# Two-layer perceiver block on one Trainium2 core: in the first head of each quad of cross attention, value projections placed in steps 3 to 8, and the splits and weighings reordered around them

## The reference, cut to what matters

```python
x = x + xattn(layernorm(x), ctx, Wq, Wk, Wv, Wo)      # x: [256, 512], ctx: [4096, 512]

def xattn(inputs_q, inputs_kv, Wq, Wk, Wv, Wo):       # H = 16 heads of HD = 128
    q = (inputs_q @ Wq).reshape(b, sq, H, HD) / sqrt(HD)
    k = (inputs_kv @ Wk).reshape(b, skv, H, HD)
    v = (inputs_kv @ Wv).reshape(b, skv, H, HD)
    attn = softmax(einsum('bqhd,bkhd->bhqk', q, k))
    return einsum('bhqk,bkhd->bqhd', attn, v).reshape(b, sq, H * HD) @ Wo
```

## Time and profile before

| | us |
|---|---|
| median of three runs | 1710.48 |
| lowest, highest | 1710.27, 1711.05 |
| the profiled execution | 1707.27 |
| its span, first to last instruction | 1705.5 |
| TensorE busy | 1649.8 (97%) |
| VectorE busy | 1090.5 (64%) |
| ScalarE busy | 694 (41%) |
| mean granted TensorE clock | 0.994 |

### The profile page before, as it was taken

How to read it: one execution, slowest core, us unless ns; L and a number is a source line. 1 busy time by engine, 2 the same in 40 slices (tenths; PEclk the granted TensorE clock), 3 DMA queues, 4 the chain that set the end, 5 groups by cost and what they waited for, 6 DMA issues and landing times.

```text
span 1705.5 us, 23514 instructions
## 1 busy us (share of the span) xinstructions
PE 1649.8 (97%) x9232; PEld 1296.6 (76%) x9232; DVE 1090.5 (64%) x1754; ACT 693.8 (41%) x938; POOL 126.6 (7%) x213
## 2 busy tenths in 40 slices
PE   8998999999999999999999999999889999999998
PEld 7887888888788888888888878888657646644444
DVE  4445777777777777777777788896554923633333
ACT  3334444544444444444444455554221312222221
POOL 0000000000000000000000001001000000011110
PEclk9999999999999999999999999999989999999999
DMA  6755454445554554545445543226210519199991
GB/s 222 206 173 152 130 136 130 126 129 137 138 140 124 136 130 123 147 136 130 121 131 140 132 120 97 93 81 216 81 50 1 197 56 421 60 381 395 396 381 48
DMA packets 117293, 270.41 MB, mean 159 GB/s; under 512 B 7168, under 2 KB 76992, under 8 KB 111040
## 3 DMA queue, kind: packets, MB, share of 16 engines
q1 hardware_dynamic: 96512, 194.45, 36.2%
q0 software_dynamic: 20672, 74.46, 14.6%
HBM read 200.69 MB, written 68.19 MB: 158 GB/s over the span
## 4 chain that ended last, share of the span: by engine, by line
PE 61%; issue 27%; DVE 4%; DMA 3%; POOL 3%; ACT 2%; SPq 0%; POOLq 0%; DVEq 0%; ACTq 0%
PE bank L41 14%; PE bank L390 13%; PE bank L362 9%; PE bank L1921 5%; PE bank L403 5%; PE bank L1551 3%; PE bank L1942 2%; PE bank L1941 2%; DMA v_dram<-v_out 2%; PE bank L1950 2%; POOL v_back L887 1%; PE bank L1906 1%; PE bank L135 1%; DMA v_out<-in_wv 1%; PE bank L1096 1%
## 5 line engine op out<-in xcount | busy, mean ns | idle before, releaser
L716 DVE TENSOR_TENSOR e_lo<-S,e_hi 128x1024 fp32r<-128x1024 f32 x128 | 156.5, 1223 | 88.8 <-ACT e_hi L548 88.4
L362 PE MATMUL bank<-cT_hi,wk_hi 128*128 128x512 f32 x512 | 205.6, 402 | 0.0
L390 PE MATMUL bank<-wv_hi,cT_hi 128*128 128x512 f32 x512 | 199.8, 390 | 3.5 <-DVE wv_lo L653 3.5
L362 PE MATMUL bank<-cT_hi,wk_lo 128*128 128x512 f32 x512 | 200.6, 392 | 0.0
L539 ACT ACTIVATE S<-S 128x1024 f32<-128x1024 f32 x128 | 135.7, 1060 | 159.6 <-DVE S L696 159.5
L390 PE MATMUL bank<-wv_hi,cT_lo 128*128 128x512 f32 x512 | 199.5, 390 | 0.0
L362 PE MATMUL bank<-cT_lo,wk_hi 128*128 128x512 f32 x512 | 199.2, 389 | 0.0
L390 PE MATMUL bank<-wv_lo,cT_hi 128*128 128x512 f32 x512 | 199.2, 389 | 0.0
L548 ACT CAST e_hi<-S 128x1024 fp32r<-128x1024 f32 x128 | 134.7, 1052 | 145.0 <-PE bank L403 141.0
L709 DVE TENSOR_TENSOR esum<-esum,S 128x512 f32<-128x512 f32 x210 | 145.0, 690 | 72.0 <-ACT S L539 68.4
L403 PE MATMUL bank<-e_hi,v_back 128*128 128x256 f32 x880 | 166.1, 286 | 8.3 <-DVE small L734 4.3
(11 more groups left out here) (280 smaller groups left out, 2851.7 us busy)
## 6 DMA issues: line engine op xcount, KB each, us to landing
w<-in_w_moe SPq DMA_DIRECT2D x32, 2304.0 KB, 11.6
v_dram<-v_out SPq DMA_DIRECT2D x112, 512.0 KB, 4.5
v_back<-v_dram POOLq DMA_DIRECT2D x110, 512.0 KB, 4.9
v_dram<-v_back SPq DMA_DIRECT2D x16, 512.0 KB, 3.9
ctx_nat<-in_ctx SPq DMA_DIRECT2D x8, 1024.0 KB, 4.9
ctx_raw<-in_ctxT SPq DMA_DIRECT2D x7, 1024.0 KB, 8.0
v_late<-v_dram POOLq DMA_DIRECT2D x14, 512.0 KB, 3.5
l_w_qkv<-in_l_wqkv SPq DMA_DIRECT2D x6, 1024.0 KB, 7.4
```

The costliest lines, as they stand in the source:

```text
L362: t = e.matmul(banks[b][:], l, r, start=(c == 0 and m == 0), stop=(c == DT - 1 and m == 2))
L390: t = e.matmul(banks[b][:], l, r, start=(c == 0 and m == 0), stop=(c == DT - 1 and m == 2))
L716: e.tensor_tensor(lo[:], Sj, hi[:].bitcast(F32), ALU.subtract).then_inc(e_split, 1)
```

## The change

In the first head of each quad (`starts_quad(h)`: h = 0, 4, 8) the units are spread differently over the steps: none in steps 0 and 1, two in step 2, one each in steps 3 to 6, two in step 7. The number of units, and every operation's work, is as before. In these heads the orders change as well:

- TensorE: `weigh(h, j-1)` comes behind `project_k(h+1, j)` and ahead of the unit, from step 3 on; `weigh(h, 1)` stands between the two units of step 2; `finish_head(h-1)` comes ahead of the scores of step 0. In h = 0 `weigh(0, 0)` comes behind the scores of step 1.
- ScalarE: `round_wv` of pieces 0 and 1 comes behind `round_e(h, 0)` and `raise_scores(h, 1)`; in each later step `round_k` and `store_scores` come ahead of `round_e`; pieces 2 and 3 come behind `raise_scores(h, 2)`.
- VectorE: `split_wv` of pieces 0 and 1 comes behind `split_e(h, 0)`, that of pieces 2 and 3 behind `keep_max(h+1, 0)`; `split_k` comes first in each step; `invert_sum(h-1)` comes earlier and `add_head(h-1)` later.

Other heads keep their order.

```diff
@@ -257,7 +257,13 @@
                 return []
             s = h % HPQ * NCH + j
             first = (h // HPQ + 1) * KVT
-            return [] if s == 0 else [first, first + 1] if s == 1 else [first + s]
+            if s < 2:
+                return []
+            return [first + u for u in ((0, 1) if s == 2 else (6, 7) if s == 7 else (s - 1,) if s < 7 else (s,))]
+
+        def starts_quad(h):
+
+            return h < LATE and h % HPQ == 0
 
         def sync_cross(e):
             def load_qo(n):
@@ -447,17 +453,23 @@
                     project_q(1)
             for h in range(LATE):
                 for j in range(NCH):
-                    if j >= 2:
+                    if j == 0 and h:
+                        weigh(h - 1, NCH - 1)
+                    elif j >= 2 and not starts_quad(h):
                         weigh(h, j - 1)
-                    elif j == 0 and h:
-                        weigh(h - 1, NCH - 1)
                     project_k(h + 1, j)
-                    if j == 1:
-                        weigh(h, 0)
-                    for u in units(h, j):
+                    if j == 0 and h and starts_quad(h):
+                        finish_head(h - 1)
+                    if h and j == 1 or j >= 3 and starts_quad(h):
+                        weigh(h, j - 1)
+                    for m, u in enumerate(units(h, j)):
                         project_v(u)
+                        if j == 2 and starts_quad(h) and m == 0:
+                            weigh(h, 1)
                     scores(h + 1, j)
-                    if j == 0 and h:
+                    if h == 0 and j == 1:
+                        weigh(0, 0)
+                    if j == 0 and h and not starts_quad(h):
                         finish_head(h - 1)
                     if j == NCH // 2:
                         project_q(h + 2)
@@ -593,22 +605,26 @@
                         for u in units(h, 0):
                             round_v(u)
                         raise_scores(h, 0)
-                        if h % HPQ == 0:
+                        round_e(h, 0)
+                        raise_scores(h, 1)
+                        if starts_quad(h):
                             round_wv(h // HPQ + 1, 0)
                             round_wv(h // HPQ + 1, 1)
-                        round_e(h, 0)
-                        raise_scores(h, 1)
                         continue
-                    if j == 1:
-                        round_k(h + 1, 1)
-                        if h % HPQ == 0:
-                            round_wv(h // HPQ + 1, 2)
-                            round_wv(h // HPQ + 1, 3)
+                    if j == 1 or starts_quad(h):
+                        round_k(h + 1, j)
+                    if starts_quad(h):
+                        store_scores(h + 1, j - 1)
                     round_e(h, j)
-                    store_scores(h + 1, j - 1)
-                    if j > 1:
-                        round_k(h + 1, j)
-                    if j == NCH - 1:
+                    if not starts_quad(h):
+                        store_scores(h + 1, j - 1)
+                        if j > 1:
+                            round_k(h + 1, j)
+                    if j == 1 and starts_quad(h):
+                        raise_scores(h, 2)
+                        round_wv(h // HPQ + 1, 2)
+                        round_wv(h // HPQ + 1, 3)
+                    elif j == NCH - 1:
                         round_wk(h + 2)
                     else:
                         raise_scores(h, j + 1)
@@ -780,27 +796,38 @@
                         for u in units(h, 0):
                             split_v(u)
                         shift(h, 1)
-                        if h % HPQ == 0:
+                        if h and starts_quad(h):
+                            invert_sum(h - 1)
+                        sum_e(h, 0)
+                        split_e(h, 0)
+                        if starts_quad(h):
                             split_wv(h // HPQ + 1, 0)
                             split_wv(h // HPQ + 1, 1)
-                        sum_e(h, 0)
-                        split_e(h, 0)
-                        if h:
+                        elif h:
                             invert_sum(h - 1)
                         continue
                     if j == 1:
+                        if h and not starts_quad(h):
+                            add_head(h - 1)
+                        if starts_quad(h):
+                            split_k(h + 1, 1)
+                            sum_e(h, 1)
+                        else:
+                            sum_e(h, 1)
+                            split_k(h + 1, 1)
+                        shift(h, 2)
+                    elif starts_quad(h):
+                        split_k(h + 1, j)
+                    split_e(h, j)
+                    keep_max(h + 1, j - 1)
+                    if j == 1 and starts_quad(h):
+                        split_wv(h // HPQ + 1, 2)
+                        split_wv(h // HPQ + 1, 3)
                         if h:
                             add_head(h - 1)
-                        sum_e(h, 1)
-                        split_k(h + 1, 1)
-                        if h % HPQ == 0:
-                            split_wv(h // HPQ + 1, 2)
-                            split_wv(h // HPQ + 1, 3)
-                        shift(h, 2)
-                    split_e(h, j)
-                    keep_max(h + 1, j - 1)
                     if j > 1:
-                        split_k(h + 1, j)
+                        if not starts_quad(h):
+                            split_k(h + 1, j)
                         if j + 1 < NCH:
                             shift(h, j + 1)
                     if j == NCH - 1:
```

## The result

The changed kernel takes 1720.63 us (median of four runs, 1718.72 to 1722.95) against 1710.76 us (median of four): ratio 1.0058, 95% interval 1.0046 to 1.0071, 9.9 us slower. The profiled execution had 1719.85 us, its span is 1718.0 us.

A forecast was written before the change was run, and what follows sets the result against it. TensorE was taken to bound the loop: gaps of 17.9 against 14.2 us (+3.7) plus slow clock (+2.6) gave +6.3 us on the median of 1710.5, so 1716.8 us, range 1708 to 1721.

The forecast's parts named there:

- What bounds the kernel: TensorE sets the loop's time; only its gaps, 14.2 us in all, can be won by a new order.
- Part 1: Steps 0 and 1: idle TensorE of 1.56, 2.6 and 0.1 us in head 0, 0.45 us in heads 4, 8.
- Part 2: Step 2's pair of units makes step 3's scores 3.9 us late (2.8 to 5.0) in heads 0, 4, 8.
- Part 3: Pair of units in step 7: the next scores 0.35 us late per head (0 to 2), where it was 0.
- Sum of the gaps: TensorE's gaps together: 17.9 us against 14.2, +3.7 us (about +0.4 to near +12).
- The clock: Slow clock behind gaps over 2.5 us: three more such gaps, half followed by 1.7 us loss, +2.6 us (0 to 6.8).
- the pair did not stay hidden: Rival claimed step 2's pair stays hidden, step 3's scores in time: -8 us, 1702.5; chance 0.11.
- trade evenly: Rival: transfers of 3.6 to 4.4 us and a clock that holds; +0.4 to +3.4 us, about 1712.5; chance 0.27.
- near case: First unit's transfer in step 2, issued close to a load of values: taken as 4.7 us (ends 3.6 and 5.8).
- the transfers alone: Transfers with no load of values close by: 4.1 and 3.6 us; 4.1 taken for step 7.
- the estimate of 3.2 us: 512 KB DMA: about 2 us plus bytes over 436 GB/s; would shorten step 3's gaps 1.5 us each, sum +1.8.

The follow-up runs named there:

- Experiment 1: Changed kernel with the round and split of the pair's second unit moved from step 2 into step 3 (heads 0, 4, 8): 1706.99 us.
- experiment 2: Changed kernel with 10 identity matmuls on TensorE ahead of the scores of step 3 in heads 0, 4, 8: 1715.02 us.
- experiment 8: Kernel before the change with 9 identity matmuls ahead of the scores of step 1 in heads 12, 13, 14: 1706.8 us.
- experiment 5: Changed kernel with the whole series of units rounded and split one place later in heads 0, 4, 8: 1708.01 us.
- experiment 3: Kernel before the change with only the new list of units, all orders as they were: 1721.22 us.
- experiment 4: Kernel of experiment 3 with step 1 mended in heads 0, 4, 8: scores copied right behind the keys' round, keys split first: 1725.01 us.
- changed kernel again: The changed kernel itself, unaltered, measured again beside the kernel before: 1720.65 us, ratio 1.0067.

## Why the prediction was right, and which term was too small

1716.8 us was forecast, with slower as the likeliest, and 1720.63 measured, inside the range of 1708 to 1721. It held narrowly: two of the four runs lie above 1721, and the likeliest band of 1714 to 1720.5 is just missed. The gaps came out as reasoned; the clock did not.

- **What bounds the kernel:** right. The gaps of TensorE and its slow clock give 9.8 of the loop's 10.8 us.
- **Part 1:** right to a few tenths. Head 0's new gap was put at 2.6 us and is 2.82 + 0.16; 0.45 for heads 4 and 8 are 0.48 + 0.16. The waits for wv_lo went. The load for head 0's second weighing (0.1 in the sum) cost nothing. A weighing late in the loop still waits 0.5 us for v_back, as one did for 0.3 before.
- **Part 2, the pair in step 2:** right. The weighing starts at 158.41 and the first unit is in v_out at 167.95, w + 9.5 (9.6 forecast); the transfer took 4.4 us (4.7 taken); the scores start at w + 16.2 (16.4). The gap is 3.7 us with its 0.16 (3.9). Experiment 1 confirms the cause.
- **Part 3:** 0.47 and 0.30 us in heads 1 and 5, under 0.2 in head 9 (0.35 each).
- **Sum of the gaps:** +4.1 us against +3.7.
- **The clock: this term was too small.** "3 x 0.5 x 1.7 = +2.6 us" took the chance of a fall from four gaps of mixed length as one half. In the two profiles of the changed kernel all six gaps of 3.5 us and more were followed by a fall, and the one of head 4 cost 2.3 us and not 1.7 both times, since the clock fell within the gap and stayed down longer. The falls cost 5.7 us by the windows and 5.6 us by experiment 2. The three gaps being nearly alike, one half was no fair value for each, and head 0's 3.58 us without a fall, which held the chance down, was one profile's luck: the same gap, 3.48 us in experiment 8, had one. The Trainium skill (TensorE: Matmul & The Clock Gate, "Why this matters for your kernels") warns of idle gaps between bursts of matmuls above a bound that the three gaps of step 3 pass and head 0's 2.8 us do not. Three falls less the one that it gives the old order would be an estimate of 2 x 1.7 = +3.4 us, and a sum of +7.1. The trace of the changed kernel agrees with it for these four gaps; the falls behind 1.9 to 2.8 us in other profiles (last section) do not.
- **The rivals:** the pair did not stay hidden, and transfers were not short enough to trade evenly. The landings of 4.4 to 4.6 us lie between the "near case" and the transfers alone; the estimate of 3.2 us from the Trainium skill (DMA: Bandwidth & Descriptors, "Anatomy of one DMA — SWDGE (gpsimd) path") was reached by none. That section is on transfers of GpSimd's queue, and the units' go by SyncE's; on GpSimd's queue the load of values took 3.5 us alone (experiment 5).

## What to carry to other kernels

An engine that works in order and waits for a transfer does no harm by waiting (6.3 us of it in experiment 1 cost TensorE 0.2 to 0.7 a head); look at what is queued behind the wait and when TensorE needs it, and put the wait behind that. When work is taken out of a step to avoid one stall, ask for everything that it covered: here the units of step 1 also covered the copy of the scores (experiment 3), and the making of e_lo and the reload of a single buffer (experiment 4). Price idle gaps of TensorE twice, for the gap and for the slow clock behind it; where a gap can't be closed, a few matmuls into an unread bank keep the clock.

## What the runs showed of the hardware that I had not expected

- Gaps of 3.48 to 4.17 us were followed by a granted clock of 0.50 in 11 of 12 cases (six in the two profiles of the changed kernel, three in experiment 4, one each in 3 and 8); the twelfth, 3.58 us in the kernel before, had none.
- Those of 2.7 us in heads 12 to 14 go either way: 25 of 30 had a fall in the ten profiles that do not fill them. Filling three of these was worth 3.7 us.
- In the loop a fall followed gaps as short as 2.48 us (changed kernel again) and 1.87 us (experiment 5), while one of 2.82 us had none. None followed the gaps of 1.68 us and less.
- The same 512 KB load of values takes 3.5 us alone and 5.5 us beside a transfer and a weight load (experiment 5), enough to make it the bound.
